# The odd-row weights of a deformable convolution, loaded tap by tap: nine transfers of 1568-byte runs in place of three of 4704

## The reference, cut to what matters

```python
om = conv3x3(x, w_off) + b_off
off_y, off_x, mask = om[:, :9], om[:, 9:18], sigmoid(om[:, 18:])
py = off_y + hs + ky
px = off_x + ws + kx
sampled = bilinear(x, py, px) * mask              # 9 taps for each pixel
out = einsum('bckhw,ock->bohw', sampled, w) + b
out = batchnorm(out)
return relu(out) + x
```

## Time and profile before

| | before |
|---|---|
| median of 3 runs | 2206.3 us (2194.02 to 2216.64) |
| the profiled execution's own time | 2216.39 us |
| its span | 2214.5 us |
| PE busy | 1464.9 us (66%) |
| DVE busy | 1555.3 us (70%) |
| ACT busy | 1208.5 us (55%) |
| packets of SP's queue q1, over the span | 73.1% of 16 DMA engines |

### The profile page before, as it was taken

How to read it: one execution, slowest core, us unless ns; L and a number is a source line. 1 busy time by engine, 2 the same in 40 slices (tenths; PEclk the granted TensorE clock), 3 DMA queues, 4 the chain that set the end, 5 groups by cost and what they waited for, 6 DMA issues and landing times. The chain is left out here.

```text
span 2214.5 us, 59304 instructions
## 1 busy us (share of the span) xinstructions
PE 1464.9 (66%) x24174; PEld 972.5 (44%) x24175; DVE 1555.3 (70%) x1718; ACT 1208.5 (55%) x1755; POOL 395.1 (18%) x743
## 2 busy tenths in 40 slices
PE   4745994000008888898889898888888888884330
PEld 4633331000005655665566666555656555552110
DVE  5335001998308998998899898887999898885215
ACT  2211224654106777776677777676777776762002
POOL 2000003665011112111111112111212211111000
PEclk9678997555558999999999999999999999997565
DMA  3087786899986999998899998988999999961008
GB/s 122 15 188 196 205 244 166 279 344 316 311 191 170 230 246 227 232 248 222 208 240 235 232 253 218 226 222 210 247 244 229 231 241 227 225 171 26 4 1 357
DMA packets 223021, 464.84 MB, mean 210 GB/s; under 512 B 65212, under 2 KB 155155, under 8 KB 219173
## 3 DMA queue, kind: packets, MB, share of 16 engines
q1 hardware_dynamic: 197200, 425.65, 73.1%
q0 software_dynamic: 20528, 21.23, 3.7%
q10 hardware_dynamic: 5030, 14.25, 2.1%
HBM read 354.00 MB, written 106.91 MB: 208 GB/s over the span
## 5 line engine op out<-in xcount | busy, mean ns | idle before, releaser
L937 PE MATMUL ps_even_v<-tent_x,stage 32*128 32x171 f32 (+3 forms) x5568 | 562.3, 328 | 156.7 <-DVE G L1059 106.0
L1059 DVE TENSOR_TENSOR G<-odd_y,ps_odd_v 128x1008 f32<-128x1008 f32 (+1 forms) x448 | 533.9, 1192 | 173.4 <-PE ps_odd_v L937 165.7
L1013 ACT COPY even_v<-ps_even_v 128x1008 f32<-128x1008 f32 (+2 forms) x464 | 450.9, 972 | 371.1 <-PE ps_odd_v L937 371.1
L937 PEld LDWEIGHTS ps_even_v<-tent_x,stage 32*128 32x128 f32 x5568 | 450.5, 192 | 310.2 <-issue 280.1
L937 PE MATMUL ps_odd_v<-tent_x,stage 32*128 32x171 f32 (+3 forms) x5568 | 564.6, 330 | 13.8 <-issue 13.8
L1067 DVE TENSOR_TENSOR G<-even_v,ps_even_y 128x1008 f32<-128x1008 f32 (+2 forms) x464 | 539.0, 1162 | 3.2 <-PE ps_even_y L912 1.3
L956 PE MATMUL ps_r<-G,conv_w 128*32 128x224 f32 (+3 forms) x9264 | 495.8, 338 | 29.6 <-issue 28.9
L937 PEld LDWEIGHTS ps_odd_v<-tent_x,stage 32*128 32x128 f32 x5568 | 442.5, 192 | 21.5 <-issue 21.5
L920 PE MATMUL ps_odd_y<-rows,sel 32*128 32x504 f32 (+1 forms) x448 | 225.1, 503 | 276.2 <-DMA rows<-scratch_parts 274.6
L868 POOL DMA_DIRECT2D scratch_conv<-res x448 | 216.4, 490 | 1013.2 <-ACT res L1020 977.3
L956 PEld LDWEIGHTS ps_r<-G,conv_w 128*32 128x32 f32 x9264 | 268.3, 110 | 201.7 <-issue 150.6
(11 more groups left out here) (158 smaller groups left out, 1037.6 us busy)
## 6 DMA issues: line engine op xcount, KB each, us to landing
place<-scratch_px SPq DMA_DIRECT2D x768, 147.0 KB, 3.6
odd_y<-scratch_full SPq DMA_DIRECT2D x192, 588.0 KB, 9.5
rows<-scratch_parts SPq DMA_DIRECT2D x192, 220.5 KB, 4.8
x<-scratch_xh SPq DMA_DIRECT2D x48, 406.0 KB, 6.1
stage<-scratch_xt SPq DMA_DIRECT2D x192, 96.0 KB, 9.3
scratch_parts<-parts SPq DMA_DIRECT2D x6, 2688.0 KB, 13.6
scratch_om<-om ACTq DMA_DIRECT2D x64, 196.0 KB, 7.2
scratch_full<-tent_y SPq DMA_DIRECT2D x12, 784.0 KB, 9.2
```

What stands on the lines that cost most here:

```text
L937: m = nc.tensor.matmul(sub(ps_v[g % 2], 0, 128, i * 512 + lo + first, dims), stage[32 * g:32 * g + 32, j * IMAGE + v * C:j * IMAGE + (v + ...
L1013: nc.scalar.copy(two(even_v[(STEPS * it + p) % 2], ROW, 2 * p), two(ps_v[0], 512, 2 * p)).then_inc(even_kept, 1)
L1059: nc.vector.tensor_tensor(sub(G, 0, 128, slot(it, v) + lo, [[ROW, 2]] + straight), weights, sub(ps_v[1], 0, 128, lo, [[512, 2]] + straight ...
```

## The change

`load_wide` issues one transfer for each tap instead of one for each three taps, and `PER_WIDE`, which the wait uses, goes from 3 to `KK` = 9. The bytes, their places in DRAM and in the tile, and the waits ahead of the first transfer are the same.

```diff
-            PER_PLACE, PER_ROWS, PER_WIDE = 12, 3, 3
+            PER_PLACE, PER_ROWS, PER_WIDE = 12, 3, KK
...
                 def load_wide(pair, n):
-                    for ky in range(3):
-                        sp.dma_start(sub(odd_y, 0, 128, (1 + n % 2) * BATCH + ky * PIECE, [[1, PIECE]]),
-                                     dram("full", (n * PAIRS + pair) * 2 * WIN * BATCH + ky * PIECE,
-                                          [[BATCH, 2 * WIN], [0, C // 2], [1, PIECE]])).then_inc(wide_loaded[n % 2], 16)
+                    for tap in range(KK):
+                        sp.dma_start(sub(odd_y, 0, 128, (1 + n % 2) * BATCH + tap * GROUP * W, [[1, GROUP * W]]),
+                                     dram("full", ((n * PAIRS + pair) * 2 * WIN * KK + tap) * GROUP * W,
+                                          [[BATCH, 2 * WIN], [0, C // 2], [1, GROUP * W]])).then_inc(wide_loaded[n % 2], 16)
```

## The result

| | before | changed |
|---|---|---|
| median of 4 runs each | 2211.47 us (2194.02 to 2220.22) | 2107.95 us (2102.41 to 2114.59) |
| span of the profiled execution | 2214.5 us | 2112.8 us |
| PE busy | 1464.9 us | 1425.9 us |
| DVE busy | 1555.3 us | 1554.0 us |
| packets of 16 DMA engines' queue q1 | 197,200 | 252,496 |

The ratio is 0.954, with a 95% interval of 0.947 to 0.961: 4.6% faster. The forecast was 2172 us in a range of 2140 to 2240.

The account below looks back on a forecast made before the run. VectorE's pace plus waits for TensorE, delayed by fetches behind `odd_y`, was taken as the bound; DMA work of 20.2 us would bind next. From 21.03 to 20.5 us over 64 batches saves 34 us: 2172 us, range 2140 to 2240.

Parts of the forecast that it names:

- What bounds the kernel: Sampling stage: VectorE sets 18.9 of 21.03 us a batch; 2.1 us idle from TensorE's instruction fetches behind `odd_y`'s backlog.
- SP's time: SP's queue: six more issues a batch, 3.6 us, covered by 7.0 us of waiting; term 0.
- DMA work: DMA engines, sampling stage: 48 more runs and 6 completions add 0.7 us, from 19.5 to 20.2 us a batch.
- One of its signs: Sign of the forecast's case: the share of DMA queue q1 rises to 92% or more.
- The backlog: `odd_y`'s queue: backlog grows 2.4 us instead of 5.2, nearly ending TensorE's gaps; up to 2 us a batch saved.
- The landing: `odd_y`'s last data land 0.7 us later, with some 2 us of room at worst; term 0.
- Rival 1: TensorE's fetches do not gain, held up by full engines as such; 2206 or 2228 us; chance 0.28.
- Rival 2: DMA engines: a 1568-byte run costs 121 ns, work becomes the bound; 49 us more, 2255; chance 0.18.
- Rival 3: DMA engines: each transfer costs 0.3 us or more of its own; about 2266 us; chance 0.03.
- Rival 4: SP slowed by full queues, 1.6 us an issue, so `odd_y` lands late; +55 us, 2261; chance 0.04.
- The low end of the forecast's own range: Whole kernel: 2135 us if fetch gaps go and runs are free, 19.8 us a batch; the case's chance 0.47.
- The rule on large transfers: `odd_y` going from 588 to 196 KB: by the skill's table, six more transfers would cost 3.6 us a batch.

Follow-up runs that it names:

- e3: Kernel before with `odd_y` in one transfer of 128 runs of 14112 bytes instead of three of 4704-byte runs; 2313.49 us, ratio 1.043.
- e1: Kernel before with the same `odd_y` bytes in eight transfers, each of 16 runs of 14112 bytes; 2222.29 us, ratio 1.005.
- k1: Kernel before with its three `odd_y` transfers spread out, the second and third waiting for the third and fourth step of a batch; 2165.75 us, ratio 0.979.
- f1: Kernel before, three `odd_y` transfers of 4704-byte runs, but each partition reads its own row (wrong numbers, only time read); 2111.22 us, ratio 0.952.
- f2: Kernel before with own rows for each partition and three `odd_y` transfers in 1568-byte runs (wrong numbers); 2115.03 us, ratio 0.953.
- f3: Changed kernel, nine `odd_y` transfers of 1568-byte runs, but each partition reads its own row (wrong numbers); 2103.61 us, ratio 0.950.
- h1: Kernel before, but the eight `odd_y` runs of an engine start 1764 bytes after one another, not at one address (wrong numbers); 2112.51 us, ratio 0.954.
- h2: Kernel before, `odd_y` rows still read eight times, but the engines' rows lie 112896 bytes apart (wrong numbers); 2214.87 us, ratio 1.001.
- h3: Kernel before with `odd_y` untouched, but `place` reads 32 different rows instead of one row 32 times (wrong numbers); ratio 0.995.

## Why the prediction was right in direction and wrong in size

- **What bounds the kernel.** Right: instruction fetches behind `odd_y`. The changed kernel has two fetches in a window where there had been none, and its gaps fell from 60.8 to 4.0 us. The prediction had this from one gap; the whole trace bears it out. Of the 47 gaps of 0.8 us or more in the kernel before, 33 end 1.2 to 1.7 us after a 16 KB packet of q8 has landed, and that packet came 10.4 us behind the one before it in the median, where 7.6 is the median of all. More than 10 us lay between two packets 30 times, in the changed kernel 7 times. Two things close the gaps, a slower entry (e3 103, e1 54; before 60.8, k1 24) and cheaper runs at the same entry (before 60.8, f1 9.6); neither orders the whole table alone. What the prediction left out is the clock: part of VectorE's idle time was not the gaps but TensorE at half clock behind them. This did not spoil the sum, since it took VectorE's whole idle time, 2.1 us a batch, for what could be gained.
- **SP's time.** Right. The nine issues take 5.7 to 7.4 us in the timeline, more than the 5.4 of the sum, and SP still waits 106.6 us at L787.
- **DMA work. This is the step that failed.** "A batch gets 48 more runs on each engine ... 54 x 13 = 0.7 us", and with it "the DMA work of 20.2 us now binds first". Measured: 18.3 us. The 13 ns for a run were not wrong as such; f2 against f1 has 0.6 us for the same 48 runs. What was missing is that the 4704-byte run of `odd_y` costs 309 ns only because eight runs begin at the same address, and that this penalty is smaller for short runs: 93 ns against 76 for 1568 bytes (changed, f2), which is some 50 ns for 4704, where the long run has 103. So a run of 1568 bytes takes 92 ns, not 108, and 24 x (309 - 276) ns are 0.8 of the 1.2 us by which the work fell. The prediction also gave all 4704-byte runs one price, "at most 295 ns", in which the dearer ones of `odd_y` do not show; single packets of the kernel before, taken apart by their order in the queue, take 271 ns for `place`, 279 for `rows` and 311 for `odd_y`. One of its signs failed accordingly: q1's share rose to 90.5%, not to 92. It had noted that a gain was "not excluded by either but nothing in the rows offers one". One row hinted at it: `place` moved 265 GB/s and `odd_y` 247, with runs of the same length. It was read as a word on many small transfers and not as a difference between two loads.
- **The backlog.** The mechanism is right, and k1 gives 2.1% for it alone. The kernel went to 19.4 us a batch, near VectorE's 18.9, and not to the 20.5 at which the prediction let the work stop it: (20.5 - 19.4) x 64 = 70 us, the 68 by which the forecast missed. The 1.6 us gained a batch lie within its "up to 2 us a batch".
- **The landing.** The forecast's sum had it 0.7 us later. From the first issue of a batch's `odd_y` to its last landing it takes 11.8 us in the median instead of 13.0, so it is 1.2 us earlier, though the last issue comes later.
- **The rivals.** Rival 1 (fetches do not gain) is refuted by the gaps. One argument against it was wrong, though: "the 10 us without a fetch" are not a wait of 10 us, since a fetch comes every 7.6 us in the median anyway. The fetches ahead of gaps were late by some 3 us, and by 5 at the most, not far from the 2.4 us of one transfer's share. Rival 2 (the work binds) had a price of 121 ns, measured 92. Rival 3 (a cost for each transfer) is refuted by f3 against f2, with six transfers more and less work. Rival 4 (SP held up) did not occur: the median issue stayed at 0.6 us.
- **A slip.** The low end of the forecast's own range, 19.8 us a batch, is 2127 us by its own sum and not 2135. The measured time lies under both.
- **The rule on large transfers.** The Trainium skill's rule to batch transfers to 1 MiB or more ("DMA: Bandwidth & Descriptors", section "Bandwidth") would have made the change a loss of 3.6 us a batch, by an estimate from its table, which is for transfers issued by GpSimd and not by SP. The trace differs, 1.6 us were gained, and e3, the one transfer of 1764 KB which follows the rule, is the slowest kernel here.

What stays open is why `odd_y`'s repeated addresses are dear, and less so in short runs, and why those of `place` are not: the traces show how long a packet took, not what it waited for, nor which engine moved it. How a late fetch comes to stand behind `odd_y` is argued from the times alone as well. How much of the changed kernel's own gain is due to the entry and how much to the cheaper run can't be split exactly, since 1568-byte runs with repeated addresses were not tried with a fast entry. The bounds are 2.1% for the entry alone (k1), and 4.8% for cheap work with the fast entry (f1).

No further version was run. f3, with 16.8 us of work and 1.1 us of gaps, took 2103.61 us, only 4 us less than the changed kernel, so cheaper transfers leave little to gain here.

## What to carry to other kernels

When the DMA engines are over 90% busy, price each load by itself and not by the mean of all runs of its length: `odd_y`, which broadcasts rows by reading them eight times, was half as dear again as with rows of its own, and shorter runs gave part of that back. `place`, which repeats rows too, was not, so a variant with distinct rows should be timed before anything is built on it. Spread a large load over time rather than entering it at once: what it delays is not only data, but also the instructions of the busiest engine. Such gaps carry no name in the waits, and they cost more than their own length here, since the granted clock was at half behind 14 of them. Neither advice is worth much where the gaps are already small (f3 is 8 us under f1), and a slower entry bought with dearer runs gave nothing (e1).

## What the runs showed of the hardware

- `odd_y`'s runs of 4704 bytes take 205 ns in a busy stretch when each row is read once (f1), and 309 when the same row is read eight times (before). A difference of 1764 bytes between the starts is enough to make them cheap (h1, 211 ns), and a larger distance between the rows changes nothing (h2, 303 ns). For `place` the same step, from one row 32 times to 32 rows, gave 0.4 us of work a batch (h3).
- The cost of 4704 repeated bytes of `odd_y` grows with the run: by the same rows 276 ns in runs of 1568, 309 in runs of 4704 and 346 in runs of 14112. Against rows read once it is some 50 ns more in runs of 1568 and 103 in runs of 4704; at 14112 no such kernel was run.
- After 1.8 MB had entered in 1.9 us, no instruction fetch of 16 KB came for 10 us, and TensorE's gaps of this kind are 1.3 us in the mean.
- After a gap of 1.75 us that ended at 1244.08 us TensorE's granted clock was 0.50 between 1246 and 1248 us and 1.00 again between 1250 and 1252. In the sampling stage of the kernel before there are 14 such stretches, 68 us in all, between 717 and 1900 us, in e3 32 with 157 us, in the changed kernel none.
